# A decoder layer in float32: q and k parts in 128 even rows, the cross value product in 64x32 tiles, and new order tables

## The reference, cut to what matters

```
x = x + attn(layernorm(x))        # 16 heads, key size 16, value size 64, softmax over axis 1 (see below)
x = x + xattn(ctx, ctx, layernorm(x))
x = x + ffn(layernorm(x))         # time shift mix, sigmoid gate, square of relu

attn:   sim  = q k^T / 4;  attn = softmax(sim, axis=1) (over the query positions);  o = attn v;  out = o W_o
xattn:  z = fm_w h + fm_b for each head h of 16 numbers;  f = [exp(z), exp(-z)]     # 32 numbers a head
        for v, k (64 context rows) and q (512 rows);  p = softmax(f_q f_k^T / 16);  out = (p f_v) W_fc + b_fc
```

## Time and profile before

| | |
|---|---|
| median of 3 runs | 481.78 us (480.9 to 482.01) |
| the profiled execution | 479.61 us, its span 477.8 us |
| PE, PEld busy | 445.1, 276.3 us |
| DVE, ACT, POOL busy | 379.9, 299.0, 134.5 us |
| value product `pv` (L795), busy | 16.5 us in 128 records |
| granted PE clock, mean | 0.98 |

### The profile page before, as it was taken

How to read it: one execution, slowest core, us unless ns; L and a number is a source line. 1 busy time by engine, 2 the same in 40 slices (tenths; PEclk the granted TensorE clock), 3 DMA queues, 4 the chain that set the end, 5 groups by cost and what they waited for, 6 DMA issues and landing times.

```text
span 477.8 us, 7930 instructions
## 1 busy us (share of the span) xinstructions
PE 445.1 (93%) x2588; PEld 276.3 (58%) x2588; DVE 379.9 (79%) x689; ACT 299.0 (63%) x732; POOL 134.5 (28%) x181
## 2 busy tenths in 40 slices
PE   7779979999999999999999999999999999896985
PEld 3553426535655676557565675566556664485774
DVE  6567676786999988886999989777999787669664
ACT  4348866577688756565796856655796668323431
POOL 2511113113623351214431442114332413142410
PEclk9979999999999999999999999999999999897999
DMA  7852210133221001323301301333102000000001
GB/s 257 309 173 108 78 68 18 45 110 123 101 86 59 12 1 34 114 68 119 105 26 47 105 6 45 113 116 118 59 16 77 36 2 0 23 0 23 2 1 44
DMA packets 20013, 34.02 MB, mean 71 GB/s; under 512 B 2308, under 2 KB 6660, under 8 KB 19844
## 3 DMA queue, kind: packets, MB, share of 16 engines
q1 hardware_dynamic: 19972, 33.52, 21.5%
HBM read 23.02 MB, written 10.49 MB: 70 GB/s over the span
## 4 chain that ended last, share of the span: by engine, by line
PE 75%; DVE 9%; issue 5%; ACT 5%; DMA 3%; POOL 1%; SPq 0%; ACTq 0%; DVEq 0%; POOLq 0%
PE av_bank L653 18%; PE m_bank L591 9%; PE m_bank L593 7%; PE m_bank L592 7%; PE s_pair L639 7%; ACT e_sb L862 4%; DVE nmax L1060 3%; PE m_bank L782 3%; PE m_bank L831 3%; DMA q_parts<-qkt_lo 3%; PE m_bank L795 3%; PE m_bank L770 2%; PE m_bank L820 2%; PE av_bank L603 2%; PE m_bank L670 2%
## 5 line engine op out<-in xcount | busy, mean ns | idle before, releaser
L862 ACT ACTIVATE e_sb<-s_pair,nmax 128x512 f32<-128x512 f32 x256 | 172.8, 690 | 55.9 <-DVE nmax L1060 55.9
L1060 DVE TENSOR_REDUCE nmax<-s_pair 128x2 f32<-128x1024 f32 x128 | 152.9, 1214 | 20.2 <-PE s_pair L639 19.3
L653 PE MATMUL av_bank<-e_sb,v_sb 128*64 128x512 f32 x512 | 124.5, 607 | 4.5 <-POOL v_sb L1330 2.4
L1330 POOL TENSOR_TENSOR v_sb<-v_sb,rsum 128x256 f32<-128x256 f32 x64 | 39.6, 619 | 179.3 <-DVE rsum L1068 169.5
L653 PEld LDWEIGHTS av_bank<-e_sb,v_sb 128*64 128x64 f32 x512 | 31.6, 136 | 57.8 <-issue 46.6
L639 PE MATMUL s_pair<-q_st,k_st 64*128 64x512 f32 x256 | 50.6, 457 | 9.5 <-issue 6.8
L862 ACT ACTIVATION_READ_ACCUMULATOR e_sb<-s_pair,nmax 128x1 f32 x256 | 53.4, 208 | 0.0
L639 PEld LDWEIGHTS s_pair<-q_st,k_st 64*128 64x128 f32 x256 | 21.2, 186 | 55.3 <-issue 35.0
L1357 POOL TENSOR_TENSOR sx<-sx,xrec 128x512 f32<-128x512 f32 x24 | 24.8, 1043 | 46.4 <-DVE xrec L1240 46.4
L591 PE MATMUL m_bank<-wo_hi,ot_hi 128*128 128x256 f32 x120 | 34.9, 291 | 0.0
L593 PE MATMUL m_bank<-wo_lo,ot_hi 128*128 128x256 f32 x120 | 33.5, 279 | 0.0
(11 more groups left out here) (179 smaller groups left out, 857.9 us busy)
## 6 DMA issues: line engine op xcount, KB each, us to landing
q_st<-q_parts SPq DMA_DIRECT2D x31, 256.0 KB, 7.7
k_st<-k_parts SPq DMA_DIRECT2D x62, 128.0 KB
q_parts<-qkt_hi SPq DMA_DIRECT2D x8, 256.0 KB
q_parts<-qkt_lo SPq DMA_DIRECT2D x8, 256.0 KB
out<-x_sb SPq DMA_DIRECT2D x8, 256.0 KB, 2.1
k_parts<-qkt_hi SPq DMA_DIRECT2D x7, 256.0 KB, 2.5
k_parts<-qkt_lo SPq DMA_DIRECT2D x7, 256.0 KB, 5.9
x_sb<-in_x SPq DMA_DIRECT2D x3, 512.0 KB, 9.1
```

The source lines that it names most:

```text
L653: mm = pe.matmul(av_bank[n % AV_BANKS][64 * par:64 * par + 64, :], v_sb[:, m, 2 * p + par, :], e_sb[:, (4 * q + 2 * i + par) % E_RING, :], ...
L862: act.activation(e_sb[:, g % E_RING, :], s_pair[k // 2][:, k % 2, :], ACT.Exp, bias=nmax[:, g % 8:g % 8 + 1], accum_out=esum[:, q % 4, k:k ...
L1060: dve.tensor_reduce(nmax[:, at:at + 2], s_pair[i][:, :, :], AX_X, ALU.max, negate=True)\
L1330: pool.tensor_tensor(v_sb[:, m:m + 2, 2 * p:2 * p + 2, :], v_sb[:, m:m + 2, 2 * p:2 * p + 2, :], rsum[:, q % 4, :].rearrange("p (m h) -> p ...
```

## The change

1. `q_parts` is laid out (head, row, part), `k_parts` (head, row, copy, part): k is stored twice, and loads take 128 consecutive rows.
2. `vblk` loses its zeros: 64 context rows by 32 columns for each head. `pv(b, half)` is one unit on PE with 16 matmuls on 64 x 32 tiles, into two banks, one for each half of the rows; ACT and DVE still evict a bank at a time. The rows of the host's `wfc` are put in the order that this gives.
3. The tables: all slots are new. `DEFER` now holds every unit of batch 2 from `op (1, 0)` and `kv` on, where it held those from `fc` on (57 entries in place of 14).
4. The warm matmuls at the start use 256 columns in place of 512.

```
-        vblk = sb("vblk", [P, NP, 2 * FE])
+        vblk = sb("vblk", [P, NP, FE])
-        q_parts = nc.dram_tensor("q_parts", (2, 8, 2, KD, N), F32, kind="Internal").ap()
-        k_parts = nc.dram_tensor("k_parts", (2, 8, KD, 2, N), F32, kind="Internal").ap()
+        q_parts = nc.dram_tensor("q_parts", (2, 8, KD, 2, N), F32, kind="Internal").ap()
+        k_parts = nc.dram_tensor("k_parts", (2, 8, KD, 2, 2, N), F32, kind="Internal").ap()
...
-                    dst = q_parts[c, :, part] if o == 0 else k_parts[c, :, :, part]
+                    if o == 0:
+                        dst = q_parts[c, :, :, part].rearrange("h k n -> (h k) n")
+                    else:
+                        dst = k_parts[c, :, :, :, part].rearrange("h k r n -> (h k) r n")
+                        src = src.unsqueeze(1).broadcast_to([P, 2, N])
                     sp.dma_start(dst, src).then_inc(stack_out[o][c], 16)
...
-                for i in range(2):
-                    k_rows = bass.AP(k_parts.tensor, k_parts[c, h + i].offset, [[0, 2], [N, 2 * KD], [1, N]])
-                    sp.dma_start(k_st[64 * i:64 * i + 64, n % STACK, :].bitcast(F32), k_rows)\
-                      .then_inc(stack_in[1][n % STACK], 16)
+                k_rows = k_parts[c, h:h + 2].rearrange("h k r p n -> (h k r p) n")
+                sp.dma_start(k_st[:, n % STACK, :].bitcast(F32), k_rows).then_inc(stack_in[1][n % STACK], 16)
...
-                cols = 512 if at < 3 else 256
+                cols = 256
...
-    if name in ("xs", "z"):
+    if name in ("xs", "z", "pv"):
...
-            def pv(b, half, gg):
+            def pv(b, half):
+                units = bank_units("pv", b, (half,))
+                for unit in units:
+                    wait_bank(pe, unit)
                 for t in (2 * half, 2 * half + 1):
-                    wait_emptied(pe, ("pt", b, (t, gg)))
+                    for gg in range(2):
+                        wait_emptied(pe, ("pt", b, (t, gg)))
                 wait_emptied(pe, ("kv", b, ()))
                 for i in range(2):
-                    for q in range(2):
-                        pair = 4 * gg + 2 * i + q
-                        mm = pe.matmul(bank(unit)[64 * q:64 * q + 64, i * HALF:(i + 1) * HALF], vblk[:, pair, :],
-                                       pt_sb[:, pair, :], start=True, stop=True)
-                mm.then_inc(filled[uses[unit][0]], 1)
+                    for c in range(4):
+                        for r, unit in enumerate(units):
+                            rows = slice(64 * r, 64 * r + 64)
+                            mm = pe.matmul(bank(unit)[32 * c:32 * c + 32, i * HALF:(i + 1) * HALF],
+                                           vblk[rows, 4 * i + c, :], pt_sb[rows, 4 * i + c, :], start=True, stop=True)
+                            if (i, c) == (1, 3):
+                                mm.then_inc(filled[uses[unit][0]], 1)
```

From the tables, the units at the start (all engines' slots of `FIRST`, `ONCE`; negative slots lie before the first scores at 12 or 13) and the quads:

```
-    ("first", (0,), dict(pe=-282, act=-235, dve=-282)),
+    ("first", (0,), dict(pe=-23, act=-338, dve=-354)),
-    ("cut", ("qk",), dict(act=-910, dve=-907)),
+    ("cut", ("qk",), dict(act=-2177, dve=-2150)),
-    ("cut", ("v1",), dict(act=-312, pool=-311)),
+    ("cut", ("v1",), dict(act=22, pool=16)),
-    ("load", ("rest",), dict(sp=-2172)),
+    ("load", ("rest",), dict(sp=28)),
-    ("cut", ("o",), dict(act=-195, pool=-202)),
+    ("cut", ("o",), dict(act=8, pool=36)),
-    ("feat", (), dict(dve=-190, act=-192)),
+    ("feat", (), dict(sp=87, dve=80, act=81)),
-ATTENTION = dict(scores=12, weigh=42, max=(11, 12), exp=(17, 17, 18, 18), rsum=27, scale=22, ot_hi=39, ot_lo=44)
+ATTENTION = dict(scores=13, weigh=43, max=(11, 11), exp=(16, 16, 17, 17), rsum=26, scale=16, ot_hi=36, ot_lo=43)
```

More of the change, by code:

```diff
@@ L201 @@
+    ("fv", (1,), dict(pe=712, dve=400, sp=731)),
 ]
 FIRST = [
-    ("warm", (0, 2), dict(pe=-1187)),
-    ("warm", (1, 2), dict(pe=-1349)),
-    ("warm", (2, 2), dict(pe=-823)),
-    ("ln1", (0,), dict(dve=-1673, pool=-1674, do=-1613)),
-    ("ln1", (1,), dict(dve=-1626, pool=-1626, do=-1460)),
-    ("cut", ("first",), dict(act=-1586, dve=-1583)),
-    ("cut", ("qk",), dict(act=-910, dve=-907)),
-    ("t1", (0,), dict(dve=-965, pe=-855, act=-966)),
-    ("t1", (1,), dict(pe=-705, act=-699, dve=-727)),
@@ L224 @@
-    ("load", ("rest",), dict(sp=-2172)),
-    ("load", ("feat",), dict(sp=-822)),
-    ("v", (0, 0), dict(pe=27, act=24)),
-    ("v", (0, 1), dict(pe=14, dve=23)),
-    ("v", (0, 2), dict(pe=-5, act=-24)),
-    ("v", (0, 3), dict(pe=15, dve=31)),
+    ("warm", (0, 2), dict(pe=-2219)),
+    ("warm", (1, 2), dict(pe=-2110)),
+    ("warm", (2, 2), dict(pe=-58)),
+    ("ln1", (0,), dict(dve=-2194, pool=-2196, do=-2188)),
+    ("ln1", (1,), dict(dve=-2189, pool=-2187, do=-2188)),
+    ("cut", ("first",), dict(act=-2215, dve=-2188)),
@@ new lines @@
+    ("cut", ("qk",), dict(act=-2177, dve=-2150)),
+    ("t1", (0,), dict(dve=-2175, pe=-2186, act=-2133)),
+    ("t1", (1,), dict(pe=-2073, act=-2074, dve=-2172)),
+    ("first", (0,), dict(pe=-23, act=-338, dve=-354)),
+    ("first", (1,), dict(pe=-11, act=-9, dve=-183)),
+    ("qk", (0, 0), dict(dve=-328, sp=-388, pe=-22, act=-292)),
+    ("qk", (0, 1), dict(pe=-14, act=-24, dve=-71, sp=-144)),
+    ("cut", ("v0",), dict(act=-1507, dve=-1507)),
+    ("cut", ("v1",), dict(act=22, pool=16)),
+    ("ld", (1,), dict(sp=-126)),
@@ L230 @@
+    ("load", ("o",), dict(sp=-1550)),
+    ("ld", (2,), dict(sp=-98)),
+    ("load", ("x1",), dict(sp=15)),
+    ("load", ("fc",), dict(sp=102)),
+    ("load", ("rest",), dict(sp=28)),
+    ("load", ("feat",), dict(sp=-435)),
+    ("v", (0, 0), dict(pe=23, act=22)),
+    ("v", (0, 1), dict(pe=21, dve=16)),
+    ("v", (0, 2), dict(pe=12, act=12)),
+    ("v", (0, 3), dict(pe=35, dve=34)),
 ]
 ONCE = [
-    ("cut", ("o",), dict(act=-195, pool=-202)),
-    ("cut", ("fc",), dict(act=267, pool=262)),
@@ L244 @@
+    ("kf", (1,), dict(pe=156, act=155)),
+    ("warm", (3, 1), dict(pe=2454)),
+    ("warm", (4, 1), dict(pe=2002)),
+    ("warm", (5, 1), dict(pe=3006)),
+    ("warm", (6, 1), dict(pe=3247)),
+    ("warm", (7, 1), dict(pe=2804)),
+    ("warm", (8, 1), dict(pe=2086)),
 ]
[L246 removed]
+ATTENTION = dict(scores=13, weigh=43, max=(11, 11), exp=(16, 16, 17, 17), rsum=26, scale=16, ot_hi=36, ot_lo=43)
@@ L990, in pt @@
                     pb, ph = (b, 0) if t >= 2 else (b - 1, 1)
-                    wait_filled(act, ("pv", pb, (ph, gg)))
+                    for r in range(2):
+                        wait_filled(act, ("pv", pb, (ph, r)))
                 elif b == 0:
@@ L1208, in kv @@
                 if b:
-                    wait_filled(dve, ("pv", b - 1, (1, 1)))
+                    for r in range(2):
+                        wait_filled(dve, ("pv", b - 1, (1, r)))
                 v4 = bank(unit)[:, :].rearrange("p (g r q s) -> p g r q s", r=2, q=2, s=FE)
```

397 lines of the change are left out of this document (215 added, 182 removed).

## The result

The changed kernel takes 468.56 us (median of four runs, 468.09 to 469.14) beside 481.61 us: a ratio of 0.9731, 95% interval 0.9714 to 0.9749, which is 2.7% faster. The forecast was 470.6 us. In a second group of runs it took 468.21 us, a ratio of 0.9759 (0.9731 to 0.9787). The profiled run took 468.09 us, 466.2 of it span; beside 479.61 and 477.8 that is 11.5 us less, where the sum of the steps said 11.2. By the medians it is 13.1 us in the first group and 11.5 in the second.

The account below looks back on a forecast made before the run. TensorE was taken as the bound, full from 160 to 410 us, with waits at the start and tail. Terms -4.0 - 5.4 - 0.8 - 1.0 = -11.2 gave 468.4 us profiled, 470.6 beside the median; range 464.5 to 481.

Parts of the forecast that it names:

- step 2: Value product: a half takes 1.07 us instead of 1.97; -5.4 us over six middle halves, -0.8 in the tail.
- step 3: DMA layout: faster q stores shorten ScalarE's wait in batch 0, -1.0 us; k loads and the doubled k store 0.
- Step 1: Start: weight splits move behind the first scores, ending TensorE's 6.17 us hole; -4.0 us, bounds -6.2 and nothing.
- Rival B: Start gives nothing: TensorE stays at low clock or ScalarE's cuts hold the exponentials; 476.1 us, chance 0.10.
- rival A: Value product: paired float32 records hold each other up, 3.66 us a half; 490.3 us, chance 0.13.
- Step 4: Tables: all slots move, with nearly the same neighbours in the middle and VectorE busy in the tail; 0 us.
- rival C: Middle: new order puts a waiting unit ahead of ready ones, 2 us a batch, +8; 478.6 us, chance 0.10.
- Rival D: Middle: VectorE holds it once TensorE is lighter, three of six halves give nothing, +2.7; 473.3 us, chance 0.07.

Follow-up runs that it names:

- the 0 to 2.3 us of `DEFER`: The changed kernel with `DEFER` cut down to its 14 old entries, the other 45 units following the plan of the other parts: 470.27 us, ratio 0.9780.
- the pair: The kernel before with the changed kernel's first units and split of o, and the new layout, without the new product and new plan: 470.97 us, ratio 0.9803.

## Why the prediction was right

The time came out 2 us below the forecast and well inside its range; 1.7 of the 2 is the 2.2 us that were added for the median, where the changed kernel's lies 0.5 above its profiled execution. The sum of the steps (11.2 of 11.5) is closer than its terms: the start gave 2.2 us more than its term, the middle 1.3 less than step 2's, and step 3's 1.0 in batch 0 did not appear. That they cancel is luck. The mechanisms of the start and of the product held; the DMA step had the wrong one.

**Step 1, -4.0, measured -6.2.** The cause held: the splits and `fm` left the front, and the hole went whole, the -6.2 end of the stated bounds. The mis-sized term is the wait for the first q store: it was priced at 4.7 us, the old landing, although step 3 of the same sum made it 2.4. It was issued at 16.8 and had landed when `qkt_hi` ran at 19.22; with the old layout that instruction ran at 21.87, and the first exponential at 24.64 in place of 22.31. That is near the 24.1 of the prediction. The short warm-up cost nothing: the first units' matmuls took 0.40 us, though the four transposes at 6.82 us took 1.11 us, where those at 7.64 in the kernel before took 0.60. The low clock that the prediction gives to the first warm unit of before was read from its pace, records 0.85 us apart beside 0.43 for the same shape from 8.08 us on; the column of the granted clock shows 1.00 in both stretches. Rival B fell. The POOL part of `cut o` did hold scaling for 0.6 us once, as bounded.

**Step 2, -5.4 and -0.8.** 1.02 to 1.10 us a half were forecast as 1.07. That eight tiles run at once was the author's estimate, since the rows of before show no more than two records at once; the trace of the changed kernel has eight started within 0.06 us, and rival A (3.66) fell with it. The 0.25 us by which the old 1.97 exceeds 8 rounds of 0.215 are put down to the change of the tile shape, which no run shows. Taking the product out again costs 4.9 to 5.2 us from quad 16 on, against 6.2 in the sum. The middle was oversized: 3.4 to 3.6 us for 5.4, and TensorE waits 1.0 us more there (8.1 from quad 16 to the last `weigh`) than with the old product (7.2). In the tail the prediction took the clock to be full; under the new tables the granted clock is 0.50 in the first half, and what the product gives there (1.66 us) only makes up for what the low clock takes (3.68 us for the old product, where it took 1.95 at 1.00).

**Step 3, -1.0: the step that failed.** It argued that the k loads are worth 0 because no load stands among TensorE's releasers, and looked only for waits that the layout ends in the old order. The k loads were slow transfers in the old order too (the trace of before has the same tail from 36 us on, below). They hid because their victim is not their reader: it is the next q store in the queue, and in the old order its reader came late (`qkt_hi` ran at 38.03 us without a wait for it). In the new order it comes early, and with the old layout it waited 7.63 us, up to 40.27. Nor did the term come true in its own place: the wait in batch 0 is gone where the layout is put on the old tables, but under the new ones 1.82 of its 2.58 us stand, because its reader comes sooner as well. So the layout is worth 3.2 us in the old order and 14 in the new one, and the start +2.4 without it and -7.0 with it (477.97 to 470.97). The sum stood because it was made for the whole change: start, layout and their interplay measure -10.2 together, where steps 1 and 3 had -5.0. Steps 2 and 4 gave some 3 us less than their terms by the medians, which hid more than half of these 5 us.

The DMA view of the kernel before, 26 to 42 us, which the prediction did not read:

```profile
DMA  7799852454489454544313593111111111111111
GB/s 100 205 346 346 207 131 74 118 87 123 179 323 312 128 133 154 172 177 174 118 72 67 189 394 128 51 51 46 51 51 51 51 51 51 51 46 51 51 51 51
```

**Step 4, 0: slightly too good.** What the pair gained over the forecast, the tables seem to have lost in part. TensorE's busy time from 160 to 410 us, of the kernel before with the pair, then of the changed kernel with the old product:

```profile
160.00:410.00 250.00, 247.78 (x1495) 153.67 (x1492) 214.68 (x392) 169.13 (x425) 75.92 (x107) 1.00 0.20 67
```
```profile
160.00:410.00 250.00, 245.97 (x1486) 154.01 (x1485) 213.04 (x394) 167.86 (x423) 77.18 (x108) 1.00 0.20 67
```

The old tables wait 2.2 us there, the new ones 4.0, and what TensorE waits for in the changed kernel (120 to 410 us) is:

```profile
PE av_bank L706 <- POOL v_sb L1389: 2.1, 2, 1.6
PE s_pair L692 <- ACT e_sb L919: 1.8, 3, 0.7
PE m_bank L806 <- DVE xt_lo L1241: 1.2, 2, 0.8
```

The 1.6 is the last `weigh`, which waited 2.0 us before; the others are single units placed ahead of their operands. This is rival C in small. Rival D's sign (VectorE over 95% beside a waiting TensorE) is there from 120 to 160 us, 38.54 of 40 us beside 1.6 us of waiting, but it was there before (38.30 and 1.5), and from 160 us on VectorE is busy 85%. But the waits do not show in the time: from quad 16 to the last `weigh` the kernel takes 304.0 us with the old tables and 303.6 with the new ones. The new tables lose in the tail, 64.4 to 66.3 us, 1.7 of it in the value product at the low clock (1.95 to 3.68). The two kernels are 470.97 and 473.39 us, from different groups, with ratios whose intervals (to 0.9832, from 0.9828) just meet; so 1.5 us (by the spans from quad 16 on) to 2.4 is likely, not shown. The start, the layout and the new product under the old tables of the other parts would be 471.0 - 5 = 466 us, an estimate from these numbers; this version was not run.

Still open: what of the 0 to 2.3 us of `DEFER` is real, why the same q store of batch 0 lands after 2.4 us in most executions with the new tables and after 4.3 to 4.4 in two, and whether other tail tables would keep the clock up.

## What to carry to other kernels

Price a transfer by everything that stands behind it in its queue, not by its reader alone: here loads that TensorE never waited for held a store for which ScalarE waited 8.46 us. Where a change moves work forward and also speeds up transfers, test the parts alone and together, since here one part was a loss by itself (+2.4 us) and the pair (-10.2) was worth three times the better one (-3.2). Use a price that one step changes in every other step that rests on it. And when two kernels are compared by stage, let the windows end at the same work, and look for waits that only one execution has before a difference is given to the edit.

## What the hardware showed that was not expected

Behind the k loads whose outermost step had two repeats the queue moved 51 GB/s, at a busy share of 0.13, where it had carried 387 GB/s at 33 us, and a q store issued behind four of them landed after 10.3 us, beside a median of 2.3 for these stores. Eight 64x32 tiles started within 0.06 us, and sixteen two-record float32 matmuls took 1.02 to 1.10 us at a granted clock of 1.00 and 1.96 at a granted clock of 0.50. k's stores, now written twice (512 KB), landed in 3.1 and 4.3 us (medians of its two parts) where the single ones of 256 KB took 2.2 and 2.5 in the same order of units, and 2.5 and 5.9 in the kernel before. So in the new order the second copy costs about 1 and 2 us of landing, and only SyncE waits for it (10.7 us in six waits), ahead of its next k load. After 6.2 us without a matmul the granted clock was 0.50 for 3.5 us of work (26.33 to 29.9 us, the old start); with dummy matmuls in that stretch it was 1.00. And the small multiply of VectorE that took 3.94 us beside GpSimd's `wo_lo` takes 0.22 in the changed kernel, where GpSimd is idle:

```profile
42.19 0.22 DVE L1231 TENSOR_SCALAR fm_sb<-fm_sb 128x128 f32<-128x128 f32 x1
```
